# Output products of a recurrent fast-weight loop with the tokens as weights, and state squares on ScalarE

## The reference, cut to what matters

```python
def step(carry, inp):
    w0_, w1_, w2_ = carry
    qi, ki, vi, lr0i, lr1i, lr2i = inp
    gate = ki @ w0_
    hb = ki @ w2_
    sg = silu(gate)
    hidden = sg * hb
    dhidden = vi @ w1_.transpose(0, 2, 1)
    ...
    w1g = newtonschulz5(jnp.einsum('bch,bcd->bhd', hidden * lr1i, vi))
    w0g = newtonschulz5(jnp.einsum('bcd,bch->bdh', ki * lr0i, dgba))
    w2g = newtonschulz5(jnp.einsum('bcd,bch->bdh', ki * lr2i, dhbm))
    w1_ = w1_ + w1g
    ...
    w0_ = w0_ / (jnp.linalg.norm(w0_, axis=1, keepdims=True) + 1e-05) * w0n
    ...
    oi = silu(qi @ w0_) * (qi @ w2_) @ w1_
    return ((w0_, w1_, w2_), oi)
```

## Time and profile before

| | |
|---|---|
| median of 3 runs | 1030.06 us (1028.35 to 1033.02) |
| span of the profiled execution, first to last instruction | 1028.6 us |
| time of the profiled execution outside its span | none is listed |
| PE busy | 970.8 us, 94% |
| DVE, ACT, POOL busy | 68%, 55%, 42% |
| granted TensorE clock, mean | 0.998 of full speed |
| steps of the recurrent loop | about 45 to 360 us of the span |

### The profile page before, as it was taken

How to read it: one execution, slowest core, us unless ns; L and a number is a source line. 1 busy time by engine, 2 the same in 40 slices (tenths; PEclk the granted TensorE clock), 3 DMA queues, 4 the chain that set the end, 5 groups by cost and what they waited for, 6 DMA issues and landing times.

```text
span 1028.6 us, 25039 instructions
## 1 busy us (share of the span) xinstructions
PE 970.8 (94%) x9714; PEld 737.7 (72%) x9714; DVE 702.0 (68%) x2121; ACT 564.1 (55%) x1450; POOL 435.5 (42%) x391
## 2 busy tenths in 40 slices
PE   5887999999999999999999999999999999999978
PEld 3566897887887755675656769786978687868546
DVE  4889988988989942213223676866686668776864
ACT  3667778777778732212223465555556556655541
POOL 1221240340541711101002666775677567779710
PEclk9999999999999999999999999999999999999999
DMA  9250000000000002900002321322132213211202
GB/s 313 68 195 2 2 0 0 0 0 0 0 2 2 2 1 48 308 1 0 1 1 51 84 61 44 72 63 52 43 73 63 52 43 72 58 37 45 92 2 84
DMA packets 32812, 52.36 MB, mean 51 GB/s; under 512 B 7760, under 2 KB 17744, under 8 KB 31824
## 3 DMA queue, kind: packets, MB, share of 16 engines
q1 hardware_dynamic: 32720, 51.10, 18.0%
HBM read 21.98 MB, written 2.10 MB: 23 GB/s over the span
## 4 chain that ended last, share of the span: by engine, by line
PE 54%; DVE 4%; ACT 2%; issue 1%
PE quad L2102 12%; PE quad L2061 10%; PE quad L1705 8%; PE quad L2119 7%; PE quad L2005 6%; PE quad L2133 5%; PE quad L2197 1%; PE quad L2069 1%; PE quad L1591 1%; ACT act_probs L2366 1%; PE quad L2024 1%; DVE act_probs L2457 1%; DVE wq_wo L2471 1%; DVE x_pairs L2487 0%; ACT act_probs L2357 0%
## 5 line engine op out<-in xcount | busy, mean ns | idle before, releaser
L2709 POOL TENSOR_TENSOR act_probs<-act_probs,rden 128x512 f32<-128x512 f32 (+3 forms) x128 | 169.0, 1327 | 111.1 <-DVE rden L2476 111.1
L2357 ACT ACTIVATE act_probs<-act_probs,neg_max 128x256 f32<-128x256 f32 (+3 forms) x256 | 140.9, 553 | 83.3 <-DVE neg_max L2457 83.1
L2061 PEld LDWEIGHTS quad<-hT,ug_queries 128*128 128x128 f32 x1024 | 122.6, 192 | 14.1 <-issue 7.7
L2061 PE MATMUL quad<-hT,ug_queries 128*128 128x128 f32 x1024 | 124.7, 275 | 0.8 <-DVE act_probs L1720 0.5
L2457 DVE CUSTOM_DVE_ANT_0 act_probs<-quad,mask 128x256 f32<-128x256 f32 (+3 forms) x256 | 115.1, 485 | 0.3 <-issue 0.3
L1705 PE MATMUL quad<-hT,ug_raw_switch 128*128 128x512 f32 x256 | 113.9, 595 | 0.0
L1720 DVE SCALAR_TENSOR_TENSOR act_probs<-quad,ws_up,silu_keys 128x512 f32<-128x512 f32 x32 | 24.0, 750 | 97.1 <-ACT silu_keys L1715 97.1
L1715 ACT ACTIVATE silu_keys<-quad,ws_gate 128x512 f32<-128x512 f32 x32 | 22.0, 687 | 118.7 <-PE quad L1705 118.7
L1705 PEld LDWEIGHTS quad<-hT,ug_raw_switch 128*128 128x128 f32 x256 | 47.5, 190 | 55.1 <-issue 54.3
L2476 DVE RECIPROCAL rden<-den 128x2 f32<-128x2 f32 x128 | 20.3, 159 | 94.2 <-ACT act_probs L2357 94.0
L2102 PE MATMUL quad<-down_raw_out,ug_raw_switch 128*128 128x256 f32 (+3 forms) x256 | 79.5, 438 | 3.6 <-DVE neg_max L2457 3.6
(11 more groups left out here) (330 smaller groups left out, 2285.7 us busy)
## 6 DMA issues: line engine op xcount, KB each, us to landing
rope_swapped<-gate SPq DMA_DIRECT2D x120, 64.0 KB, 2.0
ug_raw_switch<-gate SPq DMA_DIRECT2D x60, 128.0 KB, 2.3
ug_raw_switch<-in_wmod SPq DMA_DIRECT2D x4, 512.0 KB, 7.4
x_pairs<-in_x SPq DMA_DIRECT2D x4, 512.0 KB, 8.0
x_rows<-x_pairs SPq DMA_DIRECT2D x8, 256.0 KB, 5.0
wq_wo<-in_wq_nopeT SPq DMA_DIRECT2D x1, 2048.0 KB, 8.5
wq_wo<-in_wo SPq DMA_DIRECT2D x1, 2048.0 KB, 13.2
ug_queries<-in_switch_w SPq DMA_DIRECT2D x1, 2048.0 KB, 7.6
```

The costliest lines, as they stand in the source:

```text
L2061: mm = nc.tensor.matmul(out[:, P * i:P * i + P], w[:, kt, HP * half + i, :], k.hT[:, kt, b, cols], start=(kt == 0), stop=(kt == KT - 1))
L2357: nc.scalar.activation(tile, tile, ACT.Exp, bias=neg_max[:, r, e:e + 1], scale=-1.0, accum_out=den[:, r, e:e + 1])\
L2709: nc.gpsimd.tensor_tensor(tile, tile, rden[:, t % RING, :].unsqueeze(2).to_broadcast([P, 2, cols]), ALU.mult)\
```

## The change

Five things are done.

1. The output products are turned around: the tokens `qT` (128x64) are the stationary operand and both gate and value states of a group pair are the moving one, 256 columns, as in `gates`. `out_gate(t, i)` is four matmuls for sequence pair i into all of bank 6; two such calls replace the four `out_product` calls. `out_gate(t, 0)` stands where `out_product(0, 0)` stood, `out_gate(t, 1)` where `out_product(1, 0)` stood. `early_out` is gone. Tokens are now on partitions, so the product has to be transposed: `turn_hidden` (four transposes) stands where `out_product(1, 1)` stood. ACT takes SiLU in two halves (`silu_gate`, the second one behind the six gradient copies and ahead of the table load), DVE multiplies in two halves (`hidden_rows`, at the end of `backward`, and after the gradient sums have been taken), and ACT copies the transposed result (`take_hidden`).
2. The squares of state group 3 move from DVE to ACT, for every step but the first.
3. The second half of the query and key squares moves on DVE from behind the gradient sums to the front of the step, ahead of `backward`, for every step but the first.
4. On ACT `take_proj` moves from behind the table load to between the two state roots. In the last step POOL waits for the norm of LN0B before it moves `qT`.
5. On PE the last quarter of `project_qk` moves behind the transposes of groups 0 and 1, and the wait for all scaled states moves from ahead of `gates` to ahead of its first product with `state`.

```diff
-    SQUARED = (4, 5)
+    SQUARED, SQUARED_FIRST = (4, 5, 3), (4, 5)
...
-    G_ORDER = ((GT, 0), (SUMS, 0), (OUT_ROWS, 0), (SUMS, 1), (SUMS, 2), (GT, 2), (SUMS, 3), (SUMS, 4), (GT, 4), (SUMS, 5))
+    G_ORDER = ((GT, 0), (SUMS, 0), (OUT_GATE, 1), (SUMS, 1), (SUMS, 2), (GT, 2), (SUMS, 3), (SUMS, 4), (GT, 4), (SUMS, 5))
...
-    INNER = ((A, 0), (A, 1), (OUT_ROWS, 1), (START, 0), (A, 2), ...
+    INNER = ((A, 0), (A, 1), (TURN_HID, 0), (START, 0), (A, 2), ...
...
-    TAKEN = ((AA, 0), (START, 0), ...
+    TAKEN = ((TURN_HID, 0), (AA, 0), (START, 0), ...
...
@@ gates
                     mm.then_inc(s["gates_summed"], 1)
+                    if i == 0 and (isinstance(t, bass.RuntimeValue) or t > 0):
+                        pe.wait_ge(s["w_scaled"], Q * t)
                     for hd in range(H):
...
+            def out_gate(t, i):
+                if i == 0:
+                    pe.wait_ge(s["proj_taken"], t)
+                    pe.wait_ge(s["q_moved"], t)
+                else:
+                    pe.wait_ge(s["out_hidden"], 2 * t - 1)
+                for hd in range(H):
+                    for j in range(2):
+                        mm = nc.tensor.matmul(bank[6][C * j:C * j + C, 2 * HD * hd:2 * HD * hd + 2 * HD],
+                                              qT[:, i, hd, C * j:C * j + C], weight[:, 3 * j:3 * j + 2, H * i + hd, :],
+                                              start=True, stop=True)
+                mm.then_inc(s["out_summed"], 1)
+
+            def turn_hidden(t):
+                pe.wait_ge(s["out_hidden"], 2 * t)
+                for u in range(U):
+                    mm = nc.tensor.transpose(bank[6][:, P * u:P * u + P], h_o[:, P * u:P * u + P], k.eye[:])
+                mm.then_inc(s["o_turned"], 1)
...
-                if not first:
-                    early_out(t)
                 pe.wait_ge(s["qkv_taken"], 3 * (t + 1))
...
-                    pe.wait_ge(s["w_scaled"], Q * t)
                 gates(t)
...
                     turn_weight(t - 1, 2)
-                    begin(0, G)
-                    out_product(0, 0, 0)
+                    out_gate(t, 0)
...
                 if more:
                     turn_weight(t, 3)
                     turn_weight(t, 4)
+                    turn_weight(t, 0)
+                    turn_weight(t, 1)
                     if ahead:
                         project_qk(t + 2, 1, [1])
-                    turn_weight(t, 0)
-                    turn_weight(t, 1)
...
@@ act_program
+            def silu_gate(t, i):
+                act.wait_ge(s["out_summed"], 2 * (t - 1) + i + 1)
+                nc.scalar.activation(h_o[:, H * P * i:H * P * i + H * P].rearrange("p (h d) -> p h d", h=H),
+                                     bank[6][:].rearrange("p (h g d) -> p h g d", h=H, g=2)[:, :, 0, :], ACT.Silu).then_inc(s["out_silued"], 1)
+
+            def take_hidden(t):
+                act.wait_ge(s["o_turned"], 2 * t - 1)
+                nc.scalar.activation(hid_o[:].rearrange("p i h c -> p (i h c)"), bank[6][:], ACT.Copy).then_inc(s["hid_taken"], 1)
...
                 if not first:
-                    silu_out(t - 1)
+                    silu_gate(t, 0)
                 for n, q in enumerate(MQ):
                     if n != G_DVE:
                         take(G, g_bf, q)
+                if not first:
+                    silu_gate(t, 1)
                 load_table(ACT.Sqrt)
...
-                for q in SQUARED:
+                for q in SQUARED_FIRST if first else SQUARED:
                     square_state(q)
                 root_state(1)
+                if first:
+                    nc.scalar.activation(add[:, 0, 0:1], k.neg_half[:, 0:1], ACT.Copy).then_inc(s["proj_taken"], 1)
+                else:
+                    take_proj(t - 1)
...
                 root_state(0)
                 load_table(ACT.Silu)
-                if first:
-                    ...
-                else:
-                    take_proj(t - 1)
...
@@ dve_program
+            def hidden_rows(t, i):
+                dve.wait_ge(s["out_silued"], 2 * (t - 1) + i + 1)
+                to = h_o[:, H * P * i:H * P * i + H * P].rearrange("p (h d) -> p h d", h=H)
+                nc.vector.tensor_tensor(to, bank[6][:].rearrange("p (h g d) -> p h g d", h=H, g=2)[:, :, 1, :], to, ALU.mult)\
+                    .then_inc(s["out_hidden"], 1)
...
                 by_silu(1)
+                if not first:
+                    hidden_rows(t, 0)
...
                     square_qk(t + 1, 0, (0, 1, 2, 3))
+                    dve.wait_ge(s["qkv_acted"], 3 * (t + 1) + 2)
+                    square_qk(t + 1, 1, (0, 1, 2, 3))
...
                 nc.vector.tensor_copy(g_rows[:], bank[7][:, Q * U:2 * Q * U]).then_inc(s["g_columns_taken"], 1)
-                if more:
-                    dve.wait_ge(s["qkv_acted"], 3 * (t + 1) + 2)
-                    square_qk(t + 1, 1, (0, 1, 2, 3))
...
+                if not first:
+                    hidden_rows(t, 1)
...
                     scaled(A, a_bf, g_r2, q)
-                    if not first and n == HIDDEN:
-                        hidden_out(t - 1)
...
                     update(q)
-                    if n == 3:
+                    if first and n == 3:
                         reduce_state(3)
...
@@ pool_program
                 else:
+                    pool.wait_ge(norms.xn_done, norms.groups[LN0B].end)
                     may_move(t, first)
                     move_q()
```

More of the change, by code:

```diff
@@ L44 @@
 N_FFN = 16 * 9
-N_CONSTS = 4
+N_CONSTS = 5
 def to_bf16(v):
@@ L579, in out_rows @@
             def out_rows(c, at=6):
-                pe.wait_ge(s["out_hidden"], c + 1)
+                if at == 6:
+                    pe.wait_ge(s["hid_taken"], c + 1)
+                else:
+                    pe.wait_ge(s["out_hidden"], 2 * NCH - 1)
                 for i in range(PAIRS):
@@ L633, in turn @@
                     mm.then_inc(made[q], 1)
-                def early_out(t):
-                    pe.wait_ge(s["proj_taken"], t)
-                    pe.wait_ge(s["q_moved"], t)
-                    begin(3, G)
-                    out_product(0, 1, 0)
                 def product(ph, left, right, q, plus=None):
@@ L716, in step @@
                     else:
-                        if n == 0:
-                            pe.wait_ge(s["out_silued"], t)
-                        out_product(1, n)
+                        out_gate(t, n)
                 pe.wait_ge(s["g_columns_taken"], t + 1)
@@ L743, in step @@
                         turn_v(t + 1, 7)
+                    elif ph == TURN_HID and not first:
+                        turn_hidden(t)
                     elif ph == OUT_ROWS and not first:
-                        if n == 1:
-                            out_product(1, 1)
-                        else:
-                            out_rows(t - 1)
+                        out_rows(t - 1)
                     elif ph == YT:
@@ L837, in finish @@
                 ffn.up(pe, 0, 4)
-                pe.wait_ge(s["out_silued"], NCH)
+                pe.wait_ge(s["out_silued"], 2 * NCH - 1)
                 ffn.fold(pe, 8, bank[6])
-                pe.wait_ge(s["out_hidden"], NCH)
+                pe.wait_ge(s["out_hidden"], 2 * NCH - 1)
                 ffn.fold(pe, 9, bank[7])
@@ L1008, in step @@
                         norms.modulate(act, LN0B, n, bank[7])
+                    elif ph == TURN_HID and not first:
+                        take_hidden(t)
                     elif ph == OUT_ROWS and not first:
@@ L1042, in root_state @@
                     if j == 1:
-                        act.wait_ge(s["w_squared"], 2 * t + 2)
-                    act.wait_ge(s["w_reduced"], 4 * t + 4 - 3 * j)
+                        act.wait_ge(s["w_squared"], 3 * t + 2)
+                    if first or j == 0:
+                        act.wait_ge(s["w_reduced"], 1 if j == 1 else 3 * t + 4)
                     nc.scalar.activation(w_n[:, g], w_rows[:, g], ACT.Sqrt).then_inc(s["w_rooted"], 1)
-                for q in SQUARED:
+                for q in SQUARED_FIRST if first else SQUARED:
                     square_state(q)
                 root_state(1)
+                if first:
+                    nc.scalar.activation(add[:, 0, 0:1], k.neg_half[:, 0:1], ACT.Copy).then_inc(s["proj_taken"], 1)
+                else:
+                    take_proj(t - 1)
                 if not more:
@@ L1054, in step @@
                 load_table(ACT.Silu)
-                if first:
-                    nc.scalar.activation(add[:, 0, 0:1], k.neg_half[:, 0:1], ACT.Copy).then_inc(s["proj_taken"], 1)
-                else:
-                    take_proj(t - 1)
                 if more:
@@ L1230, in step @@
                 nc.vector.tensor_copy(g_rows[:], bank[7][:, Q * U:2 * Q * U]).then_inc(s["g_columns_taken"], 1)
-                if more:
-                    dve.wait_ge(s["qkv_acted"], 3 * (t + 1) + 2)
-                    square_qk(t + 1, 1, (0, 1, 2, 3))
```

(10 more changed lines are left out.)

21 lines of the change are left out of this document (10 added, 11 removed).

## The result

The changed kernel takes 1027.35 us (median of 20 runs, 1026.23 to 1030.34). The kernel before, in the same comparison, takes 1031.97 (20 runs, 1028.35 to 1034.34). The ratio is 0.9962, 95% interval 0.9953 to 0.9972: faster by about 3.9 us, under the 5.2 us that count as a difference here, and outside the range of 1017 to 1026.

A forecast was written before the change was run, and what follows sets the result against it. PE was taken to bound the loop (38.28 of 39 us). At -1.32 a step, steps 2 to 6 give 6.6, step 1 costs 0.2, step 7 gives 1.15, its end 0.7: 1030.06 - 8.3 = 1021.8 us, range 1017 to 1026.

The forecast's parts named there:

- Two of them: 1.80: Output products on PE: two turned calls, each priced at 0.90 us like the gates' four matmuls, cost 1.80 a step.
- 1.54: Output products and their transposes on PE: net 1.54 us less work a step, the most PE can give before its waits.
- Gates start at 166.26: Seam between steps: gates start at 166.26 against 167.12, -0.85 us a step (bounds -0.45 and -1.25).
- 0.4 credited at the seam: Seam: DVE's factor, relieved of four squares, comes 0.4 us earlier, out of a possible 0 to 0.87.
- Nothing in a step of the loop: Key squares ahead of `backward`: 0.87 us more on DVE before the slopes, on time to 0.1, so no cost.
- 0.0: Halves of the hidden product: ACT's load and root reach the total at about the same relative time, 0.0 (bounds -0.2, +0.4).
- -0.44: Newton-Schulz list on PE: transposes at 0.49 replace the second half product at 0.93, -0.44 us a step (bounds 0, -0.6).
- +0.2: Step 1: +0.87 from key squares, less 0.44 for transposes and 0.2 for squares no longer before ACT's root: +0.2 us.
- DVE and ACT become the bound: Rival, chance 0.18: the chain through DVE and ACT sets the pace, a step gains 0.7, time 1025.8 us.
- DVE late: Rival, chance 0.05: second key squares make DVE miss the slopes, +0.43 a step, 1032.4 us.
- without pairing: Rival, chance 0.02: the two 64-wide tiles run one after the other, 1.8 a call, step +0.26, 1032 us.
- The stages after the loop ... start as much earlier: Behind the loop: stages bound by PE start earlier by the whole gain of 8.3 us, with no change in length forecast.

The follow-up runs named there:

- seam_back: Changed kernel with the projection's late quarter put back ahead of the transposes of groups 0 and 1: 1028.32 us, ratio 0.9963.
- sq3_back: Changed kernel with the squares of state group 3 given back to DVE: 1031.67 us, ratio 0.9997.
- out_only: Changed kernel keeping only the turned products and POOL's new wait, its other edits undone: 1031.93 us, ratio 1.0009.
- keys_back: Changed kernel with DVE's second key squares put back behind the gradient column sums: 1030.03 us, ratio 0.9981.

## Why the prediction was wrong, point by point

- **The products' cost: mis-sized.** The step that failed is "Two of them: 1.80". Measured: 1.01 (206.80 to 207.81) and 1.02 (211.10 to 212.12). What stands ahead of them, taken as unchanged, costs more too: the state transposes 1.02 (205.78 to 206.80) instead of 0.93, the gradient transposes and the sum 0.40 (210.70 to 211.10) instead of 0.34. In the kernel before:

```profile
169.87 1.09 PE L618 MATMUL quad<-eye,state 128*128 128x128 f32 x8
...
174.61 0.40 PE L632 MATMUL quad<-eye_bf,act_probs 128*128 128x128 bf16 x4
...
174.95 1.08 PE L574 MATMUL quad<-qT,weight 128*128 128x64 f32 x8
```

  The 0.90 of the earlier trace rows was a call followed by value products that go into the same 128x64 tile. Together 0.11 + 0.12 + 0.09 + 0.06 = 0.38 of PE's work, most of the 0.45 between 1.54 and 1.09. The turned half's transposes came out as forecast (0.45, 215.08 to 215.53, against 0.49). The products do pair up: a call costs 1.0, not 1.8.
- **The seam: -0.50, not -0.85.** The step that failed is "Gates start at 166.26", 3.12 behind the transposes' start at 163.14; measured 3.50. Two terms were too small. Group 0 was to be transposed at 164.3, 1.16 behind that start; it came 1.45 behind it (199.53 to 200.98), for DVE's factor is ahead of the transposes by 1.43 (198.10) where it was by 1.21 (161.93), so 0.22 earlier and not the 0.4 taken, and PE starts 0.1 behind the scale's end. And the projection takes 0.96 (202.07 to 203.03) in front of a 128x64 tile, not 0.86. More could hardly be had by PE's order: ACT's copy of group 1, checked only as something hidden, ends 0.16 ahead of the gates, and seam_back, where the gates wait 0.79 for it, shows that moving the projection is worth 0.07. Group 0's pause was foreseen ("up to 0.4"; 0.41).
- **Third group on ACT: called hidden, with 0.4 credited at the seam.** The size was right: 0.39 a step, 0.16 of it ahead of the state transposes (24.49 against 24.33 in sq3_back) and 0.22 from there to the gates (3.72 against 3.50). ACT's root at 197.50 stands ahead of DVE's factor, as forecast. At the finish the edit is worth 1.30, though the finish as a whole gained 0.80 (forecast 0.7) and out_only, without this edit, has 47.58: the parts don't add up there, and why was not tried.
- **Key squares: "Nothing in a step of the loop".** The largest miss of reasoning. DVE did stay in time (0.19 of wait at 203.76, slopes at 204.69, no pause of PE), but what the squares stopped holding up was not looked for: ACT's root for the keys, worth 0.56 a step. The forecast looked at the root for the gradients only and put "0.0" there.
- **Turned hidden product: -0.44**, taken whole. The stretch from the total to the state transposes gave -0.82; keys_back accounts for 0.56 of it (24.89 against 24.33) and sq3_back for 0.16, which leaves 0.10, if the parts add up. In out_only PE waits 0.27 longer than before for the same bf16 copy (0.61 against 0.34): most of the 0.44 was cover for it. No run had this edit alone. ACT's root comes 0.55 behind the start of the total instead of 0.44, so 0.1 late and not 0.3.
- **Step 1.** The key squares landed on the path as told. But the -0.44 and -0.2 set against them don't exist there, since step 0 turns no hidden product. Over six executions with those squares early, the distance is 50.58 in the mean, over four of the kinds of before 49.51: +1.06, not +0.2. keys_back has 49.89, but out_only, whose key squares are late too, 50.42; so not all of it is theirs.
- **"DVE and ACT become the bound"**, at 0.18, was the nearest: 0.7 a step (measured 0.98) and 1025.8 us. It had the direction (out_only: PE's saving alone gives nothing), but took the DVE and ACT edits for costs; beside the turned products they are what pays. Rivals with DVE late or without pairing did not come.
- **The finish.** DVE's scaling meets POOL, as the forecast feared of the squares:

```profile
354.07 2.37 DVE L1336 TENSOR_TENSOR state<-state,w_f 128x512 f32<-128x512 f32 x2
...
354.13 1.76 POOL L1442 TENSOR_TENSOR proj_gated<-proj_gated,gate_pairs 128x512 f32<-128x512 f32 x1 [3.56 <-ACT proj_gated L961]
```

Two scales take 2.37 here and 1.29 elsewhere (198.56). The Trainium skill (SBUF — State Buffer, "Who interferes with whom") says that only these two engines share ports and exclude each other; the rows agree.
- **"The stages after the loop ... start as much earlier"**: the step that failed is that their own length was taken as fixed. They start earlier and take 2.6 us longer in the profiles, about 2.4 in the means; what makes them longer stays open. This and the loop's 1.9 are the two causes of the miss. A third is the base, and that is luck: the median of 3 runs was 1030.06, that of 20 is 1031.97. 1.9 + 2.6 + 1.9 less 0.3 from the start is 6.1; the forecast was off by 5.55, and the difference is scatter between executions.

## What to carry to other kernels

In a loop where three engines hand work to each other, cutting the busiest engine's work alone may give nothing, even where it is busy 98% of a step: follow each pause of the others (here 0.26 us on ACT) to what queues behind it, since an edit that ends such a pause can be worth more than the work removed from the bound. Price an instruction from a row whose neighbours have the same shape as the new ones. Before resting tenths of a per cent on a profile, see where its execution lies among the single times, and don't assume that a gain ahead of a long stage arrives whole at its end.

## What was not expected of the hardware

Going from a 128x64 tile to a 128x128 or a 64x128 one cost PE about 0.1 us each time (0.90 against 1.01; 0.44 against 0.54). The kernel before took 1028.9 us in the mean of its runs at a mean granted clock of 0.998 and 1033.4 at 0.993, but the changed kernel's 20 runs show no such order. After a wait of 3.2 us at the same instruction PE may run on at full clock or fall to 1.2 GHz, where 48 matmuls take 2.61 instead of 1.55 us. The Trainium skill (TensorE: Matmul & The Clock Gate, Part 1) says that the gate's timekeeping runs free and is not restarted by the kernel; the scatter between executions agrees, but the mean length of the stages behind the loop still changed by 1.7 us when the loop's end moved by 0.8, which that sentence alone doesn't explain.
